# AdaLN cross-attention on one core: normalisation and turning of the attention weights one step later, output projection one step later, weight sums wholly on VectorE

## What is computed

```python
def _ada_ln(x, c, W_ss, b_ss):
    mu = jnp.mean(x, axis=-1, keepdims=True)
    var = jnp.mean((x - mu) ** 2, axis=-1, keepdims=True)
    h = (x - mu) / jnp.sqrt(var + EPS)
    ss = jax.nn.silu(c) @ W_ss + b_ss
    scale, bias = jnp.split(ss, 2, axis=-1)
    return (1.0 + scale)[:, None, :] * h + bias[:, None, :]

xq = _ada_ln(x_q, t_vec, Wss_q, bss_q)
xkv = _ada_ln(x_kv, t_vec, Wss_kv, bss_kv)
q = (xq @ Wq + bq).reshape(B, Lq, nh, dh)
kv = (xkv @ Wkv + bkv).reshape(B, Lkv, 2, nh, dh)
k = kv[:, :, 0]
v = kv[:, :, 1]
scores = jnp.einsum('bqhd,bkhd->bhqk', q, k) / jnp.sqrt(jnp.float32(dh))
attn = jax.nn.softmax(scores, axis=-1)
out = jnp.einsum('bhqk,bkhd->bqhd', attn, v).reshape(B, Lq, H)
return x_q + (out @ Wp + bp)
```

## Time and profile before

| | |
|---|---|
| median of 3 executions | 1246.71 us |
| lowest to highest | 1243.78 to 1247.53 us |
| the profiled execution | 1245.6 us |
| its span, first to last instruction | 1243.7 us |
| granted TensorE clock, mean | 0.984 of full speed |
| busy share of the span: TensorE, VectorE, ScalarE, GpSimd | 94%, 84%, 72%, 76% |
| bytes moved, mean rate | 111.91 MB, 90 GB/s |

### The profile page before, as it was taken

The page is one execution under the profiler, slowest core; times in us unless marked ns, Lnnn a source line. Parts: engine busy times, 40 slices in busy tenths (PEclk is TensorE's granted clock), DMA queues, the critical chain, the costliest instruction groups (busy, mean ns, idle before and its releaser), DMA issues.

```text
span 1243.7 us, 33482 instructions
## 1 busy us (share of the span) xinstructions
PE 1167.9 (94%) x11072; PEld 691.2 (56%) x11072; DVE 1045.9 (84%) x1797; ACT 891.2 (72%) x1688; POOL 947.6 (76%) x1202
## 2 busy tenths in 40 slices
PE   7788899999999999999999999999999999999976
PEld 2564455555555555555555555555555555555543
DVE  4744889888988898888989889889889898898985
ACT  2466777787777877787777777776878777777633
POOL 2543687979798888979797988889796978888443
PEclk9798899999999999999999999999999999999998
DMA  9110132222322322223222232222322222222111
GB/s 331 51 43 26 52 103 84 97 99 79 101 84 93 101 76 101 89 88 101 83 94 100 77 101 83 94 101 76 101 83 94 101 79 98 88 89 84 60 60 52
DMA packets 59865, 111.91 MB, mean 90 GB/s; under 512 B 6412, under 2 KB 6440, under 8 KB 59832
## 3 DMA queue, kind: packets, MB, share of 16 engines
q1 hardware_dynamic: 41400, 77.92, 18.1%
q10 hardware_dynamic: 18432, 33.56, 8.7%
HBM read 77.90 MB, written 33.55 MB: 90 GB/s over the span
## 4 chain that ended last, share of the span: by engine, by line
POOL 49%; issue 35%; PE 3%; POOLq 2%; DVE 1%; ACT 1%; ACTq 0%; DVEq 0%
POOL xr L414 11%; POOL half_den L421 9%; POOL xh L381 6%; POOL w_lo L428 5%; POOL veps L367 5%; POOL xr L390 4%; POOL rstd L369 4%; POOL var L365 2%; POOLq L224 2%; POOL neg_mean L356 1%; PE ps_o L1196 1%; PE ps_q L1131 0%; POOL w_tmp L404 0%; PE ps_o L1131 0%; PE ps_t L1165 0%
## 5 line engine op out<-in xcount | busy, mean ns | idle before, releaser
L615 ACT ACTIVATE pr<-pr,exp_scale 128x1024 f32<-128x1024 f32 x128 | 147.3, 1150 | 101.4 <-DVE pr L895 101.4
L421 POOL TENSOR_TENSOR half_den<-pr 128x512 f32<-128x512 f32 x128 | 162.7, 1271 | 71.5 <-ACT pr L615 71.2
L875 DVE SCALAR_TENSOR_TENSOR pr<-pr,rden 128x512 f32<-128x512 f32 x256 | 172.5, 714 | 4.3
L390 POOL TENSOR_TENSOR xr<-xr,bp_row 128x512 f32<-128x512 f32 x128 | 162.4, 1269 | 13.2 <-POOL rstd L369 6.9
L564 ACT ACTIVATE q_hi<-ps_q,cur_bq 128x512 f16<-128x512 f32 x126 | 86.3, 685 | 119.3 <-PE ps_q L1131 118.9
L414 POOL TENSOR_TENSOR xr<-y,xr 128x512 f32<-128x512 f32 x128 | 162.9, 1272 | 10.2 <-ACT y L530 10.2
L1165 PE MATMUL ps_t<-ident,pr 128*128 128x128 f32 x1024 | 147.6, 280 | 23.5 <-DVE pr L875 23.4
L903 DVE TENSOR_TENSOR pt_lo<-ps_t,pt_hi 128x512 f16<-128x512 f32 x256 | 163.3, 678 | 1.4 <-ACT pt_hi L554 1.4
L883 DVE TENSOR_REDUCE mx<-ps_s 128x8 f32<-128x512 f32 x256 | 163.8, 680 | 0.0
L895 DVE TENSOR_TENSOR pr<-ps_s,mx 128x512 f32<-128x512 f32 x256 | 163.3, 678 | 0.0
L845 DVE TENSOR_TENSOR xT_lo<-ps_t,xT_hi 128x512 f16<-128x512 f32 x128 | 88.5, 691 | 86.5 <-ACT xT_hi L505 86.5
(11 more groups left out here) (163 smaller groups left out, 2429.2 us busy)
## 6 DMA issues: line engine op xcount, KB each, us to landing
x_in<-in_x_dram SPq DMA_DIRECT2D x128, 256.0 KB, 2.8
xr<-in_x_dram SPq DMA_DIRECT2D x128, 256.0 KB, 2.9
out_dram<-xr ACTq DMA_DIRECT2D x128, 256.0 KB, 2.3
raw<-in_L_xcond_Wss_kv_dram SPq DMA_DIRECT2D x4, 512.0 KB, 5.3
cx<-in_ctx_dram SPq DMA_DIRECT2D x1, 2048.0 KB, 12.1
raw<-in_L_xcond_Wss_q_dram SPq DMA_DIRECT2D x4, 512.0 KB, 13.0
raw<-in_L_xcond_Wkv_dram SPq DMA_DIRECT2D x2, 1024.0 KB, 15.5
wq<-in_L_xcond_Wq_dram SPq DMA_DIRECT2D x1, 1024.0 KB, 16.5
```

The lines of the kernel that those rows point to most:

```text
L390: pool.tensor_tensor(xr[:, s, :], xr[:, s, :], bp_row[:, :], ALU.add).then_inc(xr_ready, 1)
L421: pool.tensor_tensor(half_den[:, :, :], pr[:, off % 2, :, 0:LKV // 2], pr[:, off % 2, :, LKV // 2:LKV], ALU.add).then_inc(half_done, 1)
L615: act.activation(pr[:, i % 2], pr[:, i % 2], ACT.Exp, scale=exp_scale[:, 0:1]).then_inc(exp_done, 1)
L875: dve.scalar_tensor_tensor(out=pr[:, off % 2, hs, :], in0=pr[:, off % 2, hs, :], scalar=P_UNIT, in1=rden[:, hs].unsqueeze(2).to_broadcast( ...
```

## The change

In each step:

- TensorE: `turn_p` stays on unit i - 1 and goes to the end of the step; `weigh` goes from unit i - 1 to i - 2, `project_out` from i - 2 to i - 3 and ahead of `turn_x`. 
- VectorE: maxima and subtractions come ahead, then `pt_lo` of unit i - 2 (before: i - 1), then the sum, the reciprocal and the normalisation of unit i - 1, then `q_lo`. The sum is one reduction of 128 x 1024 elements of `pr`.
- GpSimd: `half_sums` is gone; `add_rows` and `residual` take units i - 4 and i - 3.
- ScalarE: the row sums come first, the copies of turned tiles ahead of the squares, `vb` in i = 2, `kb` behind `q_hi`; output, `oT_hi`, `pt_hi` and the store take the units one step older.
- PSUM: `turn_x` writes the second bank of `ps_v` once the prologue is over, `weigh` always the first; `ps_t` belongs to `turn_p`. The first batch waits for `k32_done`, since the prologue's keys used `ps_v`.
- There are four drain steps in place of three.

The diff, with the declarations of the dropped buffer and semaphore cut:

```diff
@@ -249,8 +248,12 @@
                     step(b, i)
             for i in range(PER):
                 step(B - 1, i)
-            for i in range(3):
+            for i in range(4):
                 step(B, i)
+
+        def x_bank(b, off):
+
+            return ps_t[:, 0, :] if isinstance(b, int) and unit(b, off) < PER else ps_v[:, 1, :]
 
         def place(copy, part, t):
 
@@ -413,14 +416,6 @@
                     wait(pool, xr_ready, upto(b, off))
                     pool.tensor_tensor(xr[:, s, :], y[:, off % 2, :], xr[:, s, :], ALU.add).then_inc(y_ready, 1)
 
-            def half_sums(b, off):
-
-                if exists(b, off):
-                    wait(pool, exp_done, upto(b, off))
-                    wait(pool, den_done, unit(b, off))
-                    pool.tensor_tensor(half_den[:, :, :], pr[:, off % 2, :, 0:LKV // 2], pr[:, off % 2, :, LKV // 2:LKV],
-                                       ALU.add).then_inc(half_done, 1)
-
             def scaled_wq_lo(b, m):
                 if batch_exists(b):
                     wait(pool, w_hi_done, KC * b + m + 1)
@@ -441,12 +436,11 @@
                 pool.tensor_tensor(lim_f[:, :], lim_all[:, 0:MAX_SC], one_half[:, :], ALU.pow).then_inc(lim_root, 1)
 
             def step(b, i):
-                half_sums(b, i - 1)
                 mean(b, i + 8)
-                add_rows(b, i - 3)
+                add_rows(b, i - 4)
                 moments(b, i + 8)
                 await_moments(b, i + 8)
-                residual(b, i - 2)
+                residual(b, i - 3)
                 normalise(b, i + 8)
                 if 2 <= i <= 5:
                     scaled_wq_lo(b + 1, i - 2)
@@ -502,7 +496,7 @@
                 wait(act, xT_turned, upto(b, off))
                 if off % 4 == 0:
                     wait(act, q_mm, unit(b, off - 4))
-                act.copy(xT_hi[:, s, :, cols], ps_t[:, 0, :].rearrange("p (k n) -> p k n", k=KC))\
+                act.copy(xT_hi[:, s, :, cols], x_bank(b, off).rearrange("p (k n) -> p k n", k=KC))\
                    .then_inc(xT_hi_done, 1)
 
             def turned_o(b, off):
@@ -510,7 +504,7 @@
                     return
                 wait(act, pv_mm, upto(b, off))
                 wait(act, out_mm, unit(b, off))
-                act.copy(oT_hi[:, :, :], ps_v[:, off % 2, :].rearrange("p (k n) -> p k n", k=KC)).then_inc(oT_hi_done, 1)
+                act.copy(oT_hi[:, :, :], ps_v[:, 0, :].rearrange("p (k n) -> p k n", k=KC)).then_inc(oT_hi_done, 1)
 
             def key_blocks(b):
 
@@ -589,34 +583,34 @@
                 act.copy(w_hi[:, :, m * P:(m + 1) * P], w_tmp[:, :, :]).then_inc(w_hi_done, 1)
 
             def step(b, i):
-                output(b, i - 3)
+                sum_rows(b, i + 8)
+                output(b, i - 4)
                 if not (isinstance(b, int) and b == 0 and i == 0):
                     turned_x(b, i + 7)
-                sum_rows(b, i + 8)
-                turned_o(b, i - 2)
+                turned_o(b, i - 3)
+                turned_p(b, i - 2, 0)
+                turned_p(b, i - 2, 1)
+                sum_squares(b, i + 8)
                 if isinstance(b, int) and b == 0 and i in (0, 1):
                     wp_high(i)
                 if 2 <= i <= 5:
                     scaled_wq_hi(b + 1, i - 2)
-                if i == 1:
-                    values(b)
                 if i == 4:
                     query_bias(b + 1)
+                if i == 2:
+                    values(b)
+                query(b, i + 4)
                 if i == 7:
                     key_blocks(b + 1)
-                sum_squares(b, i + 8)
-                query(b, i + 4)
-                turned_p(b, i - 1, 0)
-                turned_p(b, i - 1, 1)
                 if exists(b, i):
                     if isinstance(b, int) and b == 0 and i == 0:
                         act.wait_ge(lim_step, EXP_SCALED)
                     wait(act, sub_done, 2 * upto(b, i))
                     act.activation(pr[:, i % 2], pr[:, i % 2], ACT.Exp, scale=exp_scale[:, 0:1]).then_inc(exp_done, 1)
-                if exists(b, i - 3):
-                    s = (i - 3) % 4
-                    wait(act, y_ready, upto(b, i - 3))
-                    act.dma_start(out_units[unit(b, i - 3)], xr[:, s, :]).then_inc(stored[s], 16)
+                if exists(b, i - 4):
+                    s = (i - 4) % 4
+                    wait(act, y_ready, upto(b, i - 4))
+                    act.dma_start(out_units[unit(b, i - 4)], xr[:, s, :]).then_inc(stored[s], 16)
 
             def wp_high(part):
 
@@ -842,22 +836,22 @@
                 s = (off // 4) % 2
                 cols = slice(P * (off % 4), P * (off % 4 + 1))
                 wait(dve, xT_hi_done, upto(b, off))
-                dve.tensor_tensor(xT_lo[:, s, :, cols], ps_t[:, 0, :].rearrange("p (k n) -> p k n", k=KC),
+                dve.tensor_tensor(xT_lo[:, s, :, cols], x_bank(b, off).rearrange("p (k n) -> p k n", k=KC),
                                   xT_hi[:, s, :, cols], ALU.subtract).then_inc(xT_done, 1)
 
             def turned_o(b, off):
                 if not exists(b, off):
                     return
                 wait(dve, oT_hi_done, upto(b, off))
-                dve.tensor_tensor(oT_lo[:, :, :], ps_v[:, off % 2, :].rearrange("p (k n) -> p k n", k=KC),
+                dve.tensor_tensor(oT_lo[:, :, :], ps_v[:, 0, :].rearrange("p (k n) -> p k n", k=KC),
                                   oT_hi[:], ALU.subtract).then_inc(oT_done, 1)
 
             def weight_sums(b, off):
 
                 if exists(b, off):
-                    wait(dve, half_done, upto(b, off))
+                    wait(dve, exp_done, upto(b, off))
                     wait(dve, rden_done, unit(b, off))
-                    dve.tensor_reduce(den[:, :], half_den[:, :, :], AX_X, ALU.add).then_inc(den_done, 1)
+                    dve.tensor_reduce(den[:, :], pr[:, off % 2], AX_X, ALU.add).then_inc(den_done, 1)
 
             def denominators(b, off):
 
@@ -916,17 +910,17 @@
             def step(b, i):
                 if not (isinstance(b, int) and b == 0 and i == 0):
                     turned_x(b, i + 7)
+                turned_o(b, i - 3)
+                score_max(b, i, 0)
+                score_max(b, i, 1)
+                softmax_shift(b, i)
+                turned_p(b, i - 2, 0)
+                turned_p(b, i - 2, 1)
                 weight_sums(b, i - 1)
-                turned_o(b, i - 2)
                 denominators(b, i - 1)
                 if isinstance(b, int) and b == 0 and i in (0, 1):
                     wp_low(i)
                 normalise_p(b, i - 1)
-                score_max(b, i, 0)
-                score_max(b, i, 1)
-                softmax_shift(b, i)
-                turned_p(b, i - 1, 0)
-                turned_p(b, i - 1, 1)
                 query(b, i + 4)
 
             def wp_low(part):
@@ -1109,9 +1103,10 @@
                     return
                 wait(pe, xh_ready, upto(b, off))
                 wait(pe, xT_done, unit(b, off))
-                wait(pe, pt_done, 2 * unit(b, off - 9) + 1)
+                if isinstance(b, int) and unit(b, off) >= PER:
+                    wait(pe, k32_done, CT)
                 for k in range(KC):
-                    last = pe.transpose(ps_t[:, 0, P * k:P * (k + 1)], xh[:, off % 2, P * k:P * (k + 1)], ident[:, :])
+                    last = pe.transpose(x_bank(b, off)[:, P * k:P * (k + 1)], xh[:, off % 2, P * k:P * (k + 1)], ident[:, :])
                 last.then_inc(xT_turned, 1)
 
             def project(b, off, bank=ps_q, spare=0):
@@ -1157,8 +1152,8 @@
                     return
                 for h in range(2):
                     wait(pe, norm_done, 2 * unit(b, off) + h + 1)
-                    if h == 0:
-                        wait(pe, xT_done, upto(b, off + 8))
+                    if h == 0 and isinstance(b, int) and b == 0:
+                        wait(pe, xT_done, PER)
                     wait(pe, pt_done, 2 * unit(b, off - 1) + h + 1)
                     for g in range(4):
                         pair = 4 * h + g
@@ -1171,14 +1166,16 @@
 
                 if not exists(b, off):
                     return
+                if isinstance(b, int) and b == 0:
+                    wait(pe, k32_done, CT)
                 if off % PER == 0:
                     wait(pe, vb_done, 4 * (b + off // PER + 1))
-                wait(pe, oT_done, unit(b, off - 1))
+                wait(pe, oT_done, unit(b, off))
                 wait(pe, pt_done, 2 * upto(b, off))
                 for m in range(KC):
                     for n, (pt, part) in enumerate(((pt_hi, 0), (pt_hi, 1), (pt_lo, 0))):
                         for e in range(2):
-                            last = pe.matmul(ps_v[64 * e:64 * (e + 1), off % 2, P * m:P * (m + 1)],
+                            last = pe.matmul(ps_v[64 * e:64 * (e + 1), 0, P * m:P * (m + 1)],
```

(11 more changed lines are left out.)

## The result

The changed kernel takes 1265.91 us (median of 4 runs, 1263.86 to 1267.12) against 1247.1 for the kernel before on the same chip (1243.78 to 1247.53): 1.0155 times as long, with a 95% interval of 1.0131 to 1.0179. It is slower, by 1.6%, and not by the 4.3% of the forecast of 1300. Its profiled execution took 1267.1 us with a span of 1265.3, at a mean granted clock of 0.982 (before 0.984): of the 1.6% the clock can explain 0.2 at most.

What follows compares the result with a forecast made beforehand. TensorE was taken to bound the kernel, 8.16 of 8.60 us a step. A batch goes from 68.8 to 73.0, +59 over 14, ends −4: span 1243.7 to 1299, median 1302 rounded to 1300; range 1228 to 1318.

Steps and rivals of the forecast that it cites:

- VectorE's step becomes … 8.19, level with TensorE's 8.16: Per-step work: VectorE rises from 7.55 to 8.19 us with the wider sum; TensorE stays at 8.16.
- the 0.49 from the second half of turn_p to score: TensorE: the second half of turn_p, having waited, takes 0.49 us before score, on the path to the add.
- every buffer has its own freeing wait: TensorE's moves of weigh, turn_p and project_out: weigh needs pt_done at 5.5 us, asks at 7.0; no cost counted.
- the reduction: VectorE's sum over 1024 elements instead of 512: 1.21 us where 0.68 was, bounds 0.68 and 1.36.
- rival B: GpSimd's add falls behind the second normalisation: three steps at 8.2, a batch 69.7, total 1256 us; chance 0.20.
- the forecast's hold: GpSimd's add at 7.48, ahead of VectorE's second normalisation at 7.51, holds it until 9.29; repeating steps take 9.3 us.
- i = 1, 5, 6: Steps where the add holds the second normalisation: 9.3 us each.
- i = 0: Step after the key blocks: 8.2 + 1.3 for the copies + 1.0 for a held first normalisation = 10.5 us.
- i = 2 to 4: Weight-tile steps: w_tmp on GpSimd, in flight until 7.66, holds the first normalisation; 8.8 us each.
- i = 7: Key-block step: y comes late, so the add spares the normalisations; 8.2 us.
- The ends: First and last batch and drain: emptier steps pay for the extra drain step; between 0 and −12, taken as −4.
- The hold itself: A VectorE normalisation that meets a GpSimd two-tensor add already running ends 0.54 us after that add.

Runs made afterwards that it cites:

- run 5: Changed kernel with key block copies ahead of q_hi and squares ahead of the copies of oT and pT on ScalarE: 1214.72 us, 0.9754 of the kernel before.
- run 11: Kernel of run 5 with VectorE's sum ahead of the first maximum and the reciprocal behind it: 1206.2 us, 0.9688 of the kernel before.
- Run 12: Kernel of run 11 with turn_p ahead of weigh on TensorE, oT_lo between second maximum and subtractions on VectorE: 1188.05 us, 0.955 of the kernel before.
- run 6: Changed kernel with q_lo ahead of the normalisations on VectorE: 1333.69 us, 1.0724 of the kernel before.
- run 9: Kernel of run 5 with weigh ahead of turn_x on TensorE: 1295.42 us, 1.0404 of the kernel before.
- Run 3: Changed kernel with the key block copies ahead of q_hi on ScalarE: 1232.67 us, 0.9896 of the kernel before.
- run 2: Changed kernel with the squares ahead of the copies of oT and pT on ScalarE: 1256.62 us, 1.0093 of the kernel before.
- run 8: Changed kernel with an extra one-input copy on GpSimd between mean and the add in each step: 1325.26 us, 1.0643 of the kernel before.
- run 1: Kernel before with weigh ahead of turn_x on TensorE and nothing else: 1320.94 us, 1.0601 of the kernel before.

## Why the prediction was wrong

**The step that failed** is TensorE's side of "VectorE's step becomes … 8.19, level with TensorE's 8.16", and with it the 0.49 from the second half of turn_p to score. Both were carried over from rows in which project_out follows turn_p; "every buffer has its own freeing wait" looked at waits alone and so priced the moves of turn_p and weigh at nothing. The new order costs 8.31 a step, and 0.59 from the second half of turn_p to score. VectorE's side was right, its terms as measured: 1.204 for the reduction (taken 1.21), 0.04 for the hand-over (0.03). Runs 5, 11 and 12 show that it is the order and no hidden wait: 8.31 stays the floor when VectorE's phase changes (5, 11), and goes when weigh and score become neighbours (12).

**What follows from it.** The forecast counted from the end e of the second normalisation and had TensorE waiting for it in each step. A step i = 5 of the kernel after starts in just that way:

```profile
584.88 1.80 DVE L869 SCALAR_TENSOR_TENSOR pr<-pr,rden 128x512 f32<-128x512 f32 x2
586.73 0.42 PEld L1160 LDWEIGHTS ps_t<-ident,pr 128*128 128x128 f32 x4 [0.18 <-DVE pr L869]
587.32 0.23 PE L1145 MATMUL ps_s<-kb,q_hi 64*128 64x128 f16 x2
...
593.57 1.29 DVE L869 SCALAR_TENSOR_TENSOR pr<-pr,rden 128x512 f32<-128x512 f32 x2
594.25 1.74 POOL L417 TENSOR_TENSOR xr<-y,xr 128x512 f32<-128x512 f32 x1 [0.75 <-ACT y L524]
```

Here e is 584.88 + 1.80 = 586.68, and TensorE had waited for it. The first normalisation starts 6.89 after e (forecast 6.90), the second 7.50 (7.51), and the add 6.93 after score, as in the forecast's sum. Only score is off: 0.64 after e in place of 0.06 + 0.49 = 0.55. So the add starts at 7.57 and not at 7.48, 0.07 to 0.08 behind the second normalisation and not 0.03 ahead of it, in this step of all 14 batches. That is rival B, to which I gave 0.20, on the condition that it named: the path to the add is more than 0.04 longer. From there TensorE no longer waits, and with 8.31 against VectorE's 7.50 + 0.68 = 8.18 score falls further back: 0.77 after e in i = 6, and in i = 7 603.95 − (601.75 + 1.29) = 0.91, where it also stands in run 5. B's batch of 69.7, with 8.31 in place of 8.2 in four steps, comes to 70.1; measured is 70.16. That the phase decides is shown: with later normalisations alone (run 6) the forecast's hold is there, 9.56 to 9.59 at just i = 1, 5 and 6, and run 9 falls into the same hold in every second step.

**By terms.** i = 1, 5, 6: 24.9 against 27.9, the failed step. i = 0: 10.67 against 10.5, close in sum but not as told: VectorE waits 1.49 (taken 1.3), and the add holds the second normalisation, by 1.1, not the first, by 1.0. Run 3 gives 2.36 of it back, key blocks and hold together. i = 2 to 4: 26.24 against 26.4, w_tmp ahead of the first normalisation in all three; run 2 takes it away. i = 7: 8.31 against 8.2, the floor. Sum −2.84 a batch, 40 us over 14. The ends were taken as −4 and are +2.7: the fuller first batch did gain, but the deeper pipeline adds a step to the drain and the last steps are no emptier; run 11 shows how much is in them (9.0 us in seven steps). 1299 − 40 + 7 = 1266, against a span of 1265.3.

**The hold itself** was right in size: a normalisation that finds GpSimd at work ends 0.54 after it (in i = 0 of the kernel after the add ends at 621.68, the pair at 622.22). The quoted rule of the Trainium skill on the shared SBUF interfaces (GPSIMD Engine Reference, Key points) agrees with these rows. That sentence doesn't say what GpSimd's side must read; a copy with one input holds too (run 8).

**Where the kernel's loss is.** Of the 1.35 a batch, before against after: 3.5 of waits went (68.80 − 8 × 8.16), and 1.2 for TensorE's order, 2.4 for the key blocks and 1.3 for w_tmp came. All three lie in the order of instructions (runs 12 against 5, 3, and 2). Run 12 has none of them (and the sum split around the first maximum), and its batch is 65.31.

## What to carry to other kernels

The time of a group of matmuls belongs to its neighbour too: before reordering TensorE, list which part of the array each group uses, and keep groups on parts of the array side by side. Where VectorE reads two SBUF tensors, draw GpSimd's instructions beside it in time, not in busy shares; which of them starts first, by less than 0.1 us, decides over a microsecond a step. After moving a stage, look at what once-a-batch work now stands in front of: four copies in one step of eight made the difference between slower and faster here.

## What the runs showed of the hardware

**Changing the kind of group costs TensorE time.** Four transposes, from the first one's start to the start of what follows, take 0.437 with work on the whole array on both sides. From the whole array into a part costs about 0.095: 0.530 ahead of weigh (128\*64), 0.533 ahead of score (64\*128), and 2.683 in place of 2.590 for project_out ahead of weigh (run 9). Transposes that come from weigh cost 0.055 more, 0.492; the same 0.055 is seen in the kernel before where transposes begin after a wait. Both together make 0.588 in run 1, and 1.025 in place of 0.874 for turn_p. From weigh straight to score nothing is added: weigh takes 0.793 there and 0.792 ahead of transposes, score 0.777 either way. So parting the two costs 0.15. The Trainium skill (TensorEngine Tiling (Array Packing), Key Properties) says that changing the tiling mode drains TensorE; the traces agree on the way from the whole array into a part, and show no loss on the way from one partial mode to the other. What goes on inside the engine in that time, no run here shows.

**Whoever starts first goes, also for a copy.** An add that starts 0.02 us ahead of the second normalisation holds it for its whole length; 0.08 to 0.22 behind it is itself held, to 1.60 to 1.74 in place of 1.27. A one-input copy on GpSimd of 0.61 us does the same to VectorE (1.02 to 1.10 in place of 0.69, ended 0.54 behind the copy), and is itself held to 1.08 when it starts 0.07 behind a normalisation (run 8).
